# Part of the second head group's V made during the recurrences, with five context chunks and a fifth weight slot

## The chip, the cores and the metric

The kernel runs on one core of one Trainium2 chip. The metric is the device time of one execution in microseconds, the median of several. Lower is better.

## The reference, cut to what matters

Four layers follow each other on x (8 batches, 112 steps, 512 channels) with a context ctx (8 batches, 375 rows, 512 channels), all in float32. The first is a recurrence with gates and a feed-forward part; the second two cross-attentions and an MLP; then latents and a last attention. The change touches the first layer's recurrence and the first cross-attention:

```python
# layer 0, per batch: 32 heads of 16 channels, a state s of 16 x 16 per head
def step(s, rkvw):
    r_t, k_t, v_t, w_t = rkvw
    a = k_t[:, :, :, None] * v_t[:, :, None, :]
    out = jnp.einsum('bhk,bhkd->bhd', r_t, u * a + s)
    return (a + w_t[:, :, :, None] * s, out)
...
# layer 1: 16 heads of 128 channels; kv_in is ctx, the same for both attentions
qh = (q_in @ wq + bq).reshape(b, q_len, H, K)
kh = (kv_in @ wk + bk).reshape(b, t, H, K)
vh = (kv_in @ wv + bv).reshape(b, t, H, K)
kh = concatenate([kh, bias_k]); vh = concatenate([vh, bias_v])
weights = softmax(einsum('bqhk,bthk->bhqt', qh, kh) / scale)
return einsum('bhqt,bthk->bqhk', weights, vh) @ wo + bo
```

V depends on the context and a weight alone, not on x.

## The kernel before, in words

Matrices are multiplied in three passes of single-rate float32 (`mm3`, line 187: high x high, low x high, high x low), so each operand is kept as a high and a low part. A weight of 512 x 512 (1 MB) comes into one raw tile, ACT casts it to its high part in two halves (`act_split_weight`), POOL subtracts to get the low part (`pool_split_weight`, line 229), and both lie in one of `NSLOT` = 4 slots. `ORDER` lists the weights in the order of use, `SLOT` the slot of each; a load waits until the weight before it is split.

**The recurrences.** The batches are taken in two halves of four. In each half a loop of 64 steps (n) runs over four groups of channels, 16 steps each. In a step VectorE multiplies k by a broadcast row of v (`dve_outer`; in twelve steps POOL does it, `POOL_OUTER`) and scans the state over time (`dve_scan`, line 1127), POOL multiplies the state by r (`pool_read`, line 1306), and TensorE (PE) places the results, two steps at a time, in a bank (`pe_place`, line 685). ACT puts the first state in place (`act_init`, line 908). The v rows come by DMA from HBM, broadcast, into six tiles (`sp_spread`), issued six steps ahead by SyncE (SP), whose queue carries all of these transfers. Every engine goes through the steps in an order written out by hand: between steps stand the late products of k and r, the gate's (`GATE_AT`), the norm's transposes (`TURN_AT`), sums over heads, and the weights' splits at n = 9, 18 and 59. In the loop of 64 steps the read of step n waits for the placing of step n - 4, and the outer product and the scan's first state for the read of step n - 4.

**The fills.** In steps 13 to 60 of both halves PE also makes V of the first head group of the attention (`pe_fill`). A *fill* is one group and one batch, 376 rows of context by 512 columns, in three tiles of up to 128 rows (`KTILES`), and each tile adds over four chunks of the context. A *quantum* is one tile and one chunk: three matmuls of 512 columns. There are 12 quanta in a fill, 4 fills in a half, one quantum in each of the 48 steps. `QUANTA` gives their order: tile 0 over its four chunks, then tiles 1 and 2 together, chunk by chunk. The tiles use banks 0 and 1 in turn; ACT copies a full one to SBUF (`act_value_out`, line 427) and SP stores it to HBM (`sp_value_store`, line 457). The chunks, 188 KB for each part, lie in weight slot 3 (`CONTEXT_SLOT`), one place for each of four, and are loaded from `cx_dram` by `sp_chunk` (lines 450 and 451), once the fill before has read that place. POOL made that split of the context before the loop (`pool_cx`).

**The first attention.** 32 units, one for each of four head groups and eight batches, then as many for the second attention. `unit_steps` writes PE's order: keys of four heads, the turned probabilities of the unit before, then V's three tiles (36 matmuls of 512 columns) with the attended rows and the output product between them, then the logits. Where `made(n)` holds (the first group), the unit has no V matmuls; SP brings V back from HBM (`sp_made_values`), the logits stand on both sides of the attended rows, and V's bias is added to the attended rows (`act_attended`, `dve_attended`) by four instructions in place of one.

## Time and profile before

| | us |
|---|---|
| median of 3 runs | 3144.73 |
| lowest, highest run | 3142.94, 3148.15 |
| span of the profiled execution | 3143.0 |
| PE busy in it | 2966.0 (94%) |
| loop of the first half, first scan to last | 96.7 to 232.6 |
| loop of the second half | 311.3 to 448.3 |
| first attention, first head group | 580.3 to 743.0 |

The span runs from the first to the last instruction of the profiled execution. Which of the three runs it was is not given; its span lies 0.1 us above the lowest run and 1.7 below the median.

### The profile page before, as it was taken

The numbers are of one execution on the slowest core, as the hardware profiler recorded it, in microseconds if no ns is written. First come the engines' busy times: TensorE is split into PE (matmuls) and PEld (weight loads), VectorE is DVE, ScalarE is ACT, GpSimd is POOL, SyncE is SP. The second block draws the span as 40 slices with busy tenths as digits, with TensorE's granted clock in tenths as the row PEclk, the third lists the DMA queues.
The fourth block names the chain that finished last, engine by engine and source line by source line (L and its number), as shares of the span: only waits on it lengthen the run. The fifth ranks groups of instructions, "written<-read, shape, count | busy, mean of one in ns | idle before, by whom it ended". The sixth has DMA issues, their size and how long they took to land.

```text
span 3143.0 us, 43370 instructions
## 1 busy us (share of the span) xinstructions
PE 2966.0 (94%) x16412; PEld 2488.1 (79%) x16412; DVE 1326.3 (42%) x3062; ACT 1117.2 (36%) x2541; POOL 1030.7 (33%) x956
## 2 busy tenths in 40 slices
PE   6799888899999999999999999999989999998999
PEld 3445456888998998888989989989878877777887
DVE  4784886433333333433333333333421156563134
ACT  2333345433223222333232222232333355564332
POOL 4674674213113122222121121131245333345420
PEclk8897899999999999999999999999999999999999
DMA  6664651532122122222122222121111111111133
GB/s 214 188 195 164 199 165 44 195 119 106 60 73 106 60 73 87 73 76 78 70 93 74 73 80 73 67 106 60 53 41 67 66 45 45 43 38 58 54 114 94
DMA packets 98260, 289.75 MB, mean 92 GB/s; under 512 B 8552, under 2 KB 55144, under 8 KB 89224
## 3 DMA queue, kind: packets, MB, share of 16 engines
q1 hardware_dynamic: 97576, 286.29, 26.8%
q8 instruction: 134, 2.20, 0.3%
q10 hardware_dynamic: 480, 0.69, 0.1%
q14 instruction: 70, 0.57, 0.1%
HBM read 262.96 MB, written 23.99 MB: 91 GB/s over the span
## 4 chain that ended last, share of the span: by engine, by line
PE 74%; DVE 7%; ACT 6%; POOL 5%; issue 4%; DMA 3%; PEldq 0%; PEld 0%; SPq 0%; ACTq 0%; POOLq 0%; DVEq 0%
PE bank L189 21%; PE bank L191 20%; PE bank L190 20%; PE bank L1908 5%; POOL W_lo L229 3%; PE bank L1893 2%; DMA W_raw<-in_weights 2%; DVE max L2118 1%; ACT W_hi L220 1%; ACT prob L1996 1%; PE bank L2537 1%; DVE prob L2747 1%; PE bank L625 1%; POOL x L1306 1%; ACT prob L2652 1%
## 5 line engine op out<-in xcount | busy, mean ns | idle before, releaser
L2202 POOL TENSOR_SCALAR prob<-prob,inverse 112x376 f32<-112x376 f32 x256 | 144.3, 584 | 1275.1 <-DVE inverse L2124 1275.1
L229 POOL TENSOR_TENSOR W_lo<-W_raw,W_hi 128x1024 fp32r<-128x1024 f32 x138 | 329.1, 2408 | 159.7 <-ACT W_hi L220 156.1
L189 PE MATMUL bank<-ctx_hi,W_hi 128*128 128x376 f32 x1024 | 354.0, 346 | 6.8 <-DVE K_lo L271 4.2
L271 DVE SCALAR_TENSOR_TENSOR K_lo<-bank,vectors,K_hi 128x375 fp32r<-128x375 f32 (+1 forms) x288 | 172.8, 606 | 408.7 <-ACT K_hi L262 408.7
L190 PE MATMUL bank<-ctx_lo,W_hi 128*128 128x376 f32 x1024 | 343.7, 336 | 0.0
L191 PE MATMUL bank<-ctx_hi,W_lo 128*128 128x376 f32 x1024 | 343.2, 335 | 0.0
L189 PE MATMUL bank<-act_hi,W_hi 128*128 128x448 f32 x784 | 300.1, 383 | 10.5 <-DVE act_lo L269 3.6
L2069 DVE TENSOR_TENSOR V<-bank,bv 128x512 f32<-128x512 f32 x168 | 116.3, 692 | 433.6 <-PE bank L1908 235.4
L1996 ACT ACTIVATE prob<-bank,minus 112x376 f32<-112x376 f32 x256 | 143.7, 574 | 434.3 <-DVE minus L2121 434.3
L190 PE MATMUL bank<-act_lo,W_hi 128*128 128x448 f32 x784 | 293.2, 374 | 0.0
L191 PE MATMUL bank<-act_hi,W_lo 128*128 128x448 f32 x784 | 292.7, 373 | 0.0
L189 PE MATMUL bank<-W_hi,ctx_hi 128*128 128x512 f32 (+1 forms) x672 | 274.0, 408 | 3.1 <-DVE K_lo L271 3.1
L190 PE MATMUL bank<-W_lo,ctx_hi 128*128 128x512 f32 (+1 forms) x672 | 265.4, 395 | 0.0
L191 PE MATMUL bank<-W_hi,ctx_lo 128*128 128x512 f32 (+1 forms) x672 | 264.5, 394 | 0.0
L262 ACT ACTIVATE K_hi<-bank,vectors 128x375 fp32r<-128x375 f32 (+1 forms) x288 | 162.8, 577 | 218.2 <-PE bank L191 218.2
L189 PEld LDWEIGHTS bank<-ctx_hi,W_hi 128*128 128x128 f32 x1024 | 193.4, 189 | 11.6 <-DVE K_lo L271 8.2
L189 PEld LDWEIGHTS bank<-act_hi,W_hi 128*128 128x128 f32 x784 | 151.8, 194 | 53.8 <-issue 31.7
L190 PEld LDWEIGHTS bank<-ctx_lo,W_hi 128*128 128x128 f32 x1024 | 193.9, 189 | 0.4
L191 PEld LDWEIGHTS bank<-ctx_hi,W_lo 128*128 128x128 f32 x1024 | 193.5, 189 | 0.0
L1908 PEld LDWEIGHTS bank<-prob_T,V 128*128 128x128 f32 (+1 forms) x1536 | 180.8, 191 | 8.8 <-DVE prob_T L2075 3.9
L1908 PE MATMUL bank<-prob_T,V 128*128 128x112 f32 (+1 forms) x1536 | 181.4, 275 | 1.9 <-DVE prob_T L2075 1.9
L190 PEld LDWEIGHTS bank<-act_lo,W_hi 128*128 128x128 f32 x784 | 151.9, 194 | 14.1 <-issue 0.4
(278 smaller groups left out, 6124.1 us busy)
## 6 DMA issues: line engine op xcount, KB each, us to landing
W_raw<-in_weights SPq DMA_DIRECT2D x69, 1024.0 KB, 4.9
ctx_hi<-ctx_split SPq DMA_DIRECT2D x64, 752.0 KB, 4.3
ctx_lo<-ctx_split SPq DMA_DIRECT2D x64, 752.0 KB, 5.8
v_spread<-v_rows SPq DMA_DIRECT2D x88, 224.0 KB
att<-in_ctxT SPq DMA_DIRECT2D x16, 376.0 KB, 5.3
ctx_split<-W_hi SPq DMA_DIRECT2D x16, 376.0 KB, 3.9
ctx_split<-W_lo SPq DMA_DIRECT2D x16, 376.0 KB, 4.9
W_hi<-ctx_split SPq DMA_DIRECT2D x32, 188.0 KB, 4.3
```

What stands on the lines that cost most here:

```text
L189: nc.tensor.matmul(dst, left[0], right[0], start=first, stop=False)
L190: nc.tensor.matmul(dst, left[0], right[1], start=False, stop=False)
L191: return nc.tensor.matmul(dst, left[1], right[0], start=False, stop=last)
L220: act.copy(k.Wh[:, slot, cs, :], k.Wraw[:, cs, :]).then_inc(*k.w_high.now((n, i)))
L229: pool.tensor_tensor(k.Wl[:, slot, cs, :], k.Wraw[:, cs, :], k.Wh[:, slot, cs, :].bitcast(F32), ALU.subtract).then_inc(*k.w_low.now((n, i)))
L262: act.activation(high, src, ACT.Identity, bias=bias).then_inc(*k.banks.halving(key))
L271: dve.scalar_tensor_tensor(out=low, in0=src, scalar=bias, in1=high.bitcast(F32), op0=ALU.add, op1=ALU.subtract).then_inc(*k.banks.draining ...
L1893: m = pe.transpose(bank[0:kn, j * T:(j + 1) * T], k.Pm[:, h, k0:k0 + kn], k.ident[0:T, 0:T])
L1908: m = pe.matmul(bank[:, h * T:(h + 1) * T], k.Vt[0:kn, j, h * P:(h + 1) * P], k.PT[0:kn, h, j, :], start=j == 0, stop=j == 2)
L1996: act.activation(k.Pm[:, h, :], k.banks.tile(key)[0:T, 0:SP], ACT.Exp, bias=k.nb[:, h:h + 1], scale=SCALE1, accum_out=k.ssum[:, h:h + 1]). ...
L2069: dve.tensor_tensor(k.Vt[0:kn, j, :], k.banks.tile(key)[0:kn, :], k.bv[0:kn, j // 2, :], ALU.add).then_inc(*k.banks.draining(key))
L2202: pool.tensor_scalar(k.Pm[:, h, :], k.Pm[:, h, :], k.rsum[:, h:h + 1], 1.0, ALU.mult, ALU.mult).then_inc(*k.prob_done.now((n, h)))
```

## The change

MADE becomes 2, and `WHOLE` = 1 is the number of groups made for all batches. V of group 1 is made for batches 2, 3, 6 and 7, so a half has six fills: group 0 of batches 0 and 1, then both groups of 2 and of 3 (4 to 7 in the second half). The first two go at one quantum per step in steps 13 to 36, the others at two in steps 37 to 60. The order of quanta is now tile by tile. The context has five places in slot 3, used in rotation over batches and chunks, and each batch's chunks are loaded once for both groups; a chunk is released by the last tile of the last group. ACT and SP follow PE as before for copies; SP stores a tile one step later than ACT copies it, and loads chunks in PE's own step. Group 1's weight is loaded ahead of the first loop and split in steps 3 and 5, into slot 4, and kept; the gate's load of the first half moves into step 5, behind it. That weight is loaded again in the attention for the four units that still make V. `dynamic_dma_scratch_size=512` is given when the program is built.

```diff
-MADE = 1
-ORDER = (["v", "k", "r", "v1_0", "g", "o", "v", "r", "k"] + [f"v1_{g}" for g in range(1, MADE)] + ["g", "o", "fr", "fk"]
+MADE, WHOLE = 2, 1
+ORDER = (["v", "k", "r"] + [f"v1_{g}" for g in range(MADE)] + ["g", "o", "v", "r", "k", "g", "o", "fr", "fk"]
...
-NSLOT = 4
+NSLOT = 5
...
-SLOT = ([0, 1, 0, 2, 1, 0, 1, 1, 0] + [2] * (MADE - 1) + [0, 1, 0, 2]
-        + [3, 1, 0, 2] + [(n + 3) % NSLOT for n in range(len(ORDER) - ORDER.index("q1_1"))])
+SLOT = ([0, 1, 0] + [2, 4] + [1, 0, 1, 1, 0] + [0, 1, 0, 2]
+        + [3, 1, 0, 2] + [(n + 3) % 4 for n in range(len(ORDER) - ORDER.index(f"q1_{WHOLE}"))])
...
-FILLS = [(g, b) for g in range(MADE) for b in range(B)]
-QUANTA = [(0, c) for c in range(C)] + [(j, c) for c in range(C) for j in (1, 2)]
+def groups_of(b):
+    return 1 if b % HB < 2 else MADE
+
+FILLS = [(g, b) for b in range(B) for g in range(groups_of(b))]
+QUANTA = [(j, c) for j in range(3) for c in range(C)]
...
-QUANTA_AT = [MADE if FILL_FROM <= n < FILL_TO else 0 for half, n in POINTS]
+QUANTA_AT = [groups_of((n - FILL_FROM) // NQ) if FILL_FROM <= n < FILL_TO else 0 for half, n in POINTS]
...
+CHUNKS = 5
+
+def chunk_slot(b, c):
+    return (C * (b % HB) + c) % CHUNKS
...
+def context_chunk(k, b, c):
+    cols = slice(SP * chunk_slot(b, c), SP * (chunk_slot(b, c) + 1))
+    return [w[:, CONTEXT_SLOT].rearrange("p c d -> p (c d)")[:, cols] for w in (k.Wh, k.Wl)]
...
 def tiles_of(quanta):
-    f, q = divmod(quanta, NQ)
-    return 3 * f + (q >= 4) + (q >= 11)
+    return quanta // C
...
-        elif j == 2:
-            m.then_inc(*k.chunk_read.now((f, c)))
+        elif j == 2 and g == groups_of(b) - 1:
+            m.then_inc(*k.chunk_read.now((b, c)))
...
 def sp_fill(k, half, n):
-    for q in range(made_until((half, n), 2), made_until((half, n), 1)):
+    for q in range(made_until((half, n), 1), made_until((half, n))):
         f, q = divmod(q, NQ)
-        j, c = QUANTA[q]
-        if j == 2 and (f + 1) % PER_HALF:
-            sp_chunk(k, f + 1, c)
-    for t in range(tiles_of(made_until((half, n), 3)), tiles_of(made_until((half, n), 2))):
+        (j, c), (g, b) = QUANTA[q], FILLS[f]
+        if q == 0 and g == 0 and (b + 1) % HB:
+            sp_chunk(k, b + 1, 0)
+        if j == 2 and g == groups_of(b) - 1 and (b + 1) % HB and c < C - 1:
+            sp_chunk(k, b + 1, c + 1)
+    for t in range(tiles_of(made_until((half, n), 2)), tiles_of(made_until((half, n), 1))):
         sp_value_store(k, t)
...
+def chunk_before(b, c):
+    i = C * (b % HB) + c - CHUNKS
+    return (b // HB * HB + i // C, i % C) if i >= 0 else None
...
+VALUES_AT = (3, 5)
...
+            if half == 0 and n in VALUES_AT:
+                act_split_weight(k, W_VALUES[1], (VALUES_AT.index(n),))
...
+            if half == 0 and n in VALUES_AT:
+                pool_split_weight(k, W_VALUES[1], (VALUES_AT.index(n),))
...
             sp_load_weight(k, W_VALUES[0])
             sp_cx_pass(k, 4, 8)
+            sp_load_weight(k, W_VALUES[1])
...
-        sp_load_weight(k, w["g"])
+        if half:
+            sp_load_weight(k, w["g"])
...
+            if half == 0 and n == VALUES_AT[1]:
+                sp_load_weight(k, w["g"])
...
 def made(n):
-    return n < MADE * B
+    return UNITS[n] in FILLS
...
-        pe.wait_ge(k.vt_loaded, 32 * (n + 1))
+        pe.wait_ge(k.vt_loaded, 32 * (made_before(n) + 1))
...
-    nc = _bacc.Bacc("TRN2", target_bir_lowering=False, num_devices=1)
+    nc = _bacc.Bacc("TRN2", target_bir_lowering=False, num_devices=1, dynamic_dma_scratch_size=512)
```

## Rows read from the trace of the kernel before

**Rows 1.** The page, its first part.
```profile
PE 2966.0 (94%) x16412; PEld 2488.1 (79%) x16412; DVE 1326.3 (42%) x3062; ACT 1117.2 (36%) x2541; POOL 1030.7 (33%) x956
```
**Rows 2.** Busy time by stretch of the recurrences; columns as in the first line.
```profile
core 0: us, PE busy (x) PEld busy (x) DVE busy (x) ACT busy (x) POOL busy (x), PEclk, DMA share, GB/s
...
118.46:178.40 59.94, 46.51 (x172) 23.70 (x172) 50.81 (x77) 19.59 (x54) 40.41 (x36) 0.89 0.64 195
178.40:226.60 48.20, 44.53 (x195) 24.84 (x193) 43.73 (x59) 24.07 (x59) 38.28 (x35) 0.96 0.62 193
...
396.89:443.90 47.01, 42.70 (x187) 24.04 (x186) 42.91 (x59) 22.84 (x56) 36.69 (x34) 0.96 0.62 198
```
**Rows 3.** PE's waits, 178.4 to 226.6, then 396.9 to 443.9: total, times, longest.
```profile
PE bank L189 <- DMA W_lo<-ctx_split: 3.2, 2, 1.9
...
PE bank L189 <- DMA W_lo<-ctx_split: 3.8, 2, 2.8
```
**Rows 4.** Busy time by stretch, first and third group of the first attention.
```profile
580.30:743.00 162.70, 154.15 (x914) 144.78 (x913) 60.10 (x199) 67.70 (x186) 37.23 (x46) 0.98 0.38 133
966.90:1188.80 221.90, 220.34 (x1237) 199.89 (x1236) 74.65 (x189) 63.23 (x152) 46.12 (x50) 1.00 0.21 78
```
**Rows 5.** Timeline of PE in the first recurrence, two quanta in a row: start, duration.
```profile
173.76 0.39 PE L191 MATMUL bank<-W_hi,W_lo 128*128 128x512 f32 x1
173.99 0.40 PE L189 MATMUL bank<-W_hi 128*120 128x512 f32 x1
```
**Rows 6.** Timeline of PE in the third group: twelve matmuls of a V tile.
```profile
1033.28 0.40 PE L189 MATMUL bank<-W_hi,ctx_hi 128*120 128x512 f32 x1
...
1036.06 0.36 PE L189 MATMUL bank<-act_hi,W_hi 128*128 128x448 f32 x1
```
**Rows 7.** PE's waits in the first group, 590 to 745.
```profile
PE bank L189 <- DVE K_lo L271: 4.2, 4, 2.3
PE bank L189 <- POOL W_lo L229: 2.6, 1, 2.6
PE bank L1908 <- DVE prob_T L2075: 1.9, 7, 0.3
PE bank L189 <- DVE o_lo L2083: 0.9, 3, 0.3
```
**Rows 8.** A split on POOL (lines, 96 to 119), and the timelines of POOL and VectorE.
```profile
L229 POOL TENSOR_TENSOR W_lo<-W_raw,W_hi 128x1024 fp32r<-128x1024 f32 x2 | 4.7, 2392 | 0.0
...
116.75 2.08 POOL L1306 TENSOR_TENSOR x<-tmp,rT 128x448 f32<-128x448 f32 x2
...
115.02 1.09 DVE L1127 TENSOR_TENSOR_SCAN state<-bank,state 128x452 f32<-128x452 f32 x1
```
**Rows 9.** Weight loads issued at 90.22 and 116.82: KB, us to landing.
```profile
W_raw<-in_weights SPq DMA_DIRECT2D x1, 1024.0 KB, 5.0
...
W_raw<-in_weights SPq DMA_DIRECT2D x1, 1024.0 KB, 11.5
```
**Rows 10.** Low parts of chunks: the one of 179.08, and the eight of 168 to 212.
```profile
W_lo<-ctx_split SPq DMA_DIRECT2D x1, 188.0 KB, 8.1
...
W_lo<-ctx_split SPq DMA_DIRECT2D x8, 188.0 KB, 6.7
```
**Rows 11.** Busy time of the stretch behind the wait at 187.24.
```profile
188.10:191.50 3.40, 3.40 (x9) 1.62 (x9) 1.42 (x3) 3.31 (x8) 1.20 (x2) 0.50 0.53 200
```
**Rows 12.** Timeline of PE about steps 26, 27 and 37 of the first half.
```profile
158.58 0.76 PE L189 MATMUL bank<-W_hi 128*128 128x512 f32 x1 [4.33 <-ACT value_rows L427]
...
163.65 1.21 PE L685 MATMUL bank<-y,place 128*32 128x448 f32 x4
...
178.62 0.95 PE L685 MATMUL bank<-x,place 128*32 128x448 f32 x4
```
**Rows 13.** Timeline of PE at the end of the second half: the last three placings.
```profile
444.75 0.94 PE L685 MATMUL bank<-x,place 128*32 128x448 f32 x4
449.39 0.95 PE L685 MATMUL bank<-y,place 128*32 128x448 f32 x4 [3.70 <-POOL y L1306]
451.80 1.71 PE L685 MATMUL bank<-x,place 128*32 128x448 f32 x4 [1.47 <-POOL x L1306]
```

More of the change, by code:

```diff
@@ L69 @@
 W_FFN = {w: ORDER.index(w) for w in ("fr", "fk", "fv")}
-W_X = [{w: ORDER.index(f"{w}{layer}_{g}") for w in ("qko" if layer == 1 and g < MADE else "qkvo")}
+W_X = [{w: ORDER.index(f"{w}{layer}_{g}", W_FFN["fv"]) for w in ("qko" if layer == 1 and g < WHOLE else "qkvo")}
        for layer in (1, 2) for g in range(G)]
@@ L217, in act_split_weight, with pool_split_weight @@
         act.wait_ge(*k.banks.filled(("vf", len(FILLS) - 1, 2)))
-    for i in range(2):
+    for i in parts:
         cs = slice(2 * i, 2 * i + 2)
         act.copy(k.Wh[:, slot, cs, :], k.Wraw[:, cs, :]).then_inc(*k.w_high.now((n, i)))
-def pool_split_weight(k, n):
+def pool_split_weight(k, n, parts=range(2)):
     if n >= len(ORDER):
@@ L225, in pool_split_weight @@
     pool, slot = k.nc.gpsimd, SLOT[n]
-    for i in range(2):
+    for i in parts:
         cs = slice(2 * i, 2 * i + 2)
@@ L442, in sp_first_chunk, with sp_chunk @@
             k.nc.sync.wait_ge(k.cx_stored[s], 32 * 4 * (half + 1))
-    sp_chunk(k, PER_HALF * half, c)
-def sp_chunk(k, f, c):
-    sp, b = k.nc.sync, f % B
-    if f % PER_HALF:
-        sp.wait_ge(*(k.chunk_read[f - 1, c] if c < C - 1 else k.banks.filled(("vf", f - 1, 2))))
-    ch, cl = context_chunk(k, c)
-    sp.dma_start(ch.bitcast(F32), k.cx_dram[b, 0, :, c]).then_inc(k.chunk_loaded[c], 16)
-    sp.dma_start(cl.bitcast(F32), k.cx_dram[b, 1, :, c]).then_inc(k.chunk_loaded[c], 16)
+    sp_chunk(k, HB * half, c)
+def chunk_before(b, c):
+    i = C * (b % HB) + c - CHUNKS
+    return (b // HB * HB + i // C, i % C) if i >= 0 else None
+def sp_chunk(k, b, c):
+    sp, before = k.nc.sync, chunk_before(b, c)
+    if before:
+        b0, c0 = before
+        sp.wait_ge(*(k.chunk_read[before] if c0 < C - 1 else k.banks.filled(("vf", FILLS.index((groups_of(b0) - 1, b0)), 2))))
+    ch, cl = context_chunk(k, b, c)
+    sp.dma_start(ch.bitcast(F32), k.cx_dram[b, 0, :, c]).then_inc(k.chunk_loaded[chunk_slot(b, c)], 16)
+    sp.dma_start(cl.bitcast(F32), k.cx_dram[b, 1, :, c]).then_inc(k.chunk_loaded[chunk_slot(b, c)], 16)
 def sp_value_store(k, n):
@@ L1774, in made, with made_before, value_units @@
 def made(n):
-    return n < MADE * B
+    return UNITS[n] in FILLS
+def made_before(n):
+    return sum(made(m) for m in range(n))
+def value_units(gg):
+    return [n for n in range(8 * gg, 8 * gg + 8) if not made(n)]
 def unit_steps(n):
@@ L2249, in sp_xattn @@
     sp_made_values(k, 0)
[L2250 removed]
+    sp_value_bias(k, WHOLE)
     sp_context(k, 1)
@@ L2254, in sp_xattn @@
     for n, (gg, b) in enumerate(UNITS):
-        if b == 0 and gg > MADE:
+        if b == 0 and gg > WHOLE:
             sp_value_bias(k, gg)
@@ L3247, in semaphores @@
     k.zeroed, k.first_zeroed = sem("zeroed"), sem("first_zeroed")
-    k.chunk_loaded, k.vb_loaded = [sem(f"chunk_loaded{c}") for c in range(C)], [sem(f"vb_loaded{i}") for i in range(SPREADS)]
+    k.chunk_loaded, k.vb_loaded = [sem(f"chunk_loaded{c}") for c in range(CHUNKS)], [sem(f"vb_loaded{i}") for i in range(SPREADS)]
     k.value_kept, k.v_kept = [sem("value_kept0"), sem("value_kept1")], [sem(f"v_kept{i}") for i in range(4)]
```

35 lines of the change are left out of this document (18 added, 17 removed).

## The prediction

> **What bounds the kernel now.** I began with the page: TensorE (PE) is busy 94% of a span of 3143.0 us [rows 1]. That is an average, and the change only touches two stages, so I read each by itself. The metric is the median of the runs, 3144.73 us; the profiled execution is summed against its span, 3143.0 us, which lies 1.7 us below that median, and I carry the difference through. About 0.2% (6.3 us) is what a measurement of this kernel can tell from no change.
>
> *The two recurrences* are read in busy time by stretch [rows 2], cut at the scans of steps 13, 37 and 61. In steps 13 to 36 (59.94 us in the first half) VectorE is busiest, 50.81 us, against PE's 46.51. In steps 37 to 60 (48.20 and 47.01 us), where the change adds its work, PE is busy 44.53 and 42.70 us, and what it waits for there is nearly all one thing, the low part of a context chunk: 3.2 us in the first half, 3.8 in the second [rows 3]. So there is almost no hole in PE into which a second quantum per step could go.
>
> *The first attention* (512 keys by 4 heads, eight groups of heads, eight batches each) is read by comparing the group whose V is already made (the first, 162.70 us in that stretch) with one that makes its own (the third, 221.90 us): PE is busy 154.15 and 220.34 us [rows 4]. Both are PE's; the made group has more idle time.
>
> **What the change moves, and what it costs.** One quantum is three matmuls of 512 columns. When one quantum follows another on PE, the matmuls start 0.23 us apart even across the border (173.76, then 173.99) [rows 5], so one more quantum in a step costs 0.70 us. The change adds 24 in steps 37 to 60 of each half: 24 x 0.70 = 16.8 us per half, **+33.6 us**, since PE is full there and becomes the bound by a wide margin (44.5 + 16.8 = 61.3 us against VectorE's 43.7).
>
> In the attention four units of the second group (batches 2, 3, 6, 7) lose 36 such matmuls each. There twelve of them in a row take 1033.28 to 1036.06, 0.232 us each [rows 6]: 36 x 0.232 = 8.35 us, four times, **-33.4 us**. The matmuls thus cancel, and the sum is made of the waits.
>
> (1) *Made units have less cover.* In the first group PE waits 1.9 us in 7 pieces for the turned probabilities, 4.2 us for the low keys, 0.9 us in 3 pieces for the attended rows and 2.6 us for a weight's low part [rows 7]; the third group's stretch is idle for 221.90 - 220.34 = 1.6 us in all [rows 4]. For four made units I take four pieces of the first (1.1), four of the third (1.2), two short ones of the second (0.9), and at the end of the group (batch 7 is made, as in the first group) the weight wait of 2.6 and 0.9 behind it in place of those 1.6 (1.9), plus 1.7 us for one more stretch at half clock, as the first group's PEclk of 0.98 over 162.70 us shows two such, 3.3 us of lost clock [rows 4]. **+6.8 us**; bounds 3 (the waits without weight and clock) and 8.5 (all of the first group's idle time, 162.70 - 154.15, for half as many units).
>
> (2) *The early split.* The weight for group 1's V is split in steps 3 and 5 of the first recurrence, and the load of the gate's weight moves behind it, to step 5 of SyncE's queue, where it waits for the second part of the split. ACT has room for the two copies. POOL does not: half a split takes 2.39 us [rows 8], and from step 4 on its reads pile up. Step by step: its read and outer product of step 3 end at 104.6; the half split, reads 4 and 5 (1.07 us each) and the other half end at 111.4, and reads 6 to 9 follow without a hole, to 115.5. The gate's load can be issued only at 111.4, where before it went out ahead of the loop; 1 MB lands 5.0 us after issue when the queue is empty and 11.5 when it is in traffic [rows 9]. ACT waits for it in step 9 and splits to 119, so that scan 12 starts at 119.3 against 115.02, and POOL's read 10 at 122.8 against 116.75 [rows 8]. The spreads queued behind that wait on SyncE land late as well (that of step 13 at about 122). VectorE has no hole until step 17 in which to take it back. **+4.3 us**, in the first half alone; bounds 1 (what POOL adds, less VectorE's idle) and 6.1 (read 10).
>
> (3) *Chunks.* Before, a chunk's slot was free four steps before its next use and PE still waited [rows 3]. Now three of four chunks of the next batch are released only by the last tile of the last group, and their use comes five quanta later. With two quanta a step that is two steps. From the release of the last chunk to its use I count, at the passage from one quantum a step to two (steps 35 to 38): the rest of step 36 0.8 us, a placing of 0.87, a gate product of 0.6 and three quanta, 3.7 us after the placing, so 4.5 in all. At the passage from batch 2 to 3 (steps 48 to 50) it is 5.3 us. The low part of a batch's last chunk lands 8.1 us after its issue (some 0.4 us after the release), and 6.7 us is the median of eight [rows 10]. That gives waits of about 4.0 and 3.0 us, 7.0 per half, against 3.2 and 3.8 now: +3.8 and +3.2. I add 1 us per half for one more stretch at half clock: after the wait of 1.9 us PE ran at 0.50 of its clock (1.2 GHz) for 3.4 us [rows 11]. **+9.0 us**; bounds 0 and 15. By the Trainium skill (DMA: Bandwidth & Descriptors, Anatomy of one DMA — SWDGE (gpsimd) path) a software-issued transfer takes about 2.0 us and its bytes at 436 GB/s, by which I estimate 2.4 us for 188 KB; nothing would then wait, and this term would be -7.0. The trace disagrees by a factor of three for these SyncE copies in traffic, and the measurement decides.
>
> (4) *What it gives back.* The old order began tile 2 one quantum after tile 0 was full, and PE stood 4.3 us for ACT's copy at step 26, and then ran at half clock: 0.76 us for the next matmul, where 0.40 is usual [rows 5, 12]. In the new order each bank has four quanta to be emptied. The placing of step 27, at 163.65, then comes at about 158.5, when ACT is through with the same step's table loads and root (PE's wait ended at 158.58); VectorE sets the pace to step 37, whose placing comes at 174.7 instead of 178.62 [rows 12]. **-3.9 us per half, -7.8**; bounds -2 and -10. At the end of the loop the other engines are ahead of PE. In the second half the last three placings stand at 444.75, 449.39 and 451.80, with 3.7 and 1.5 us of waiting [rows 13]; POOL's split now lies under PE's steps 57 to 60, and the last placing ends 3.9 us after that of step 61 instead of 8: -4.0. In the first half the low-rank products fill that place: -0.7. **-4.7**; bounds -1.4 and -6.
>
> The other edits cost nothing that lasts: six more value copies on ACT per half (24.07 of 48.20 us busy there [rows 2]) and six stores on SyncE, covered while PE is the bound; SyncE now waits for PE's own step before it issues the spread seven steps ahead, and VectorE can lead PE by six steps at most, so without that lead the spreads would be what is late. One weight more is loaded.
>
> Sum: 33.6 - 33.4 + 6.8 + 4.3 + 9.0 - 7.8 - 4.7 = **+7.8 us**: a span of 3150.8 and a time of **3152.5 us**.
>
> **Rivals.** *A, the chunks come in time* (the load on the queue per us falls as the steps get longer): term 3 is about 0, so 7.8 - 9.0 = -1.2, 3143.5 us. For it: the share of the DMA engines, 0.62 in steps 37 to 60 [rows 2], leaves room. Against: the 8.1 us was measured at that share.
> *B, the waits shrink everywhere*, the side of faster: PE's order without its hole at step 26 is what decides; it wins if term 3 is 0 and terms 1 and 2 are at their lower bounds: 0.2 + 3 + 1 - 7.8 - 4.7 = -8.3, 3136.4 us. The point from which it decides: added waits of terms 1 to 3 together under 6.3 us.
> *C, PE has room after all.* PE's weight loads are busy only 24.84 of 48.20 us in steps 37 to 60, against 199.89 of 221.90 in the attention [rows 2, 4]. If the loads measured its load, 16.8 us would fit into the 23 left and the whole -33.4 us would be gained: 3152.5 - 33.6 = 3118.9. The Trainium skill says so (Perfetto Trace Analysis, Identifying the Most-Contended Engine: the busy share of the weight loads tells headroom, that of matmuls does not). Against it: these matmuls are wide, starts are 0.23 us apart back to back, and the weight loads wait under them [rows 5].
> *D, ACT is late with the tiles* at two quanta per step, as at step 26 before: it has two table loads in each of steps 40 and 56. One such wait of 4.3 us and its slow clock per half: +12, 3165 us. Against: a bank now has two steps, about 5 us.
>
> **Chances.** Forecast 0.48 (of it a fifth inside 0.2%), A 0.24, B 0.14, C 0.03, D 0.11. Faster: B and C, 0.17. Within 0.2% (3138.4 to 3151.0): A and a fifth of the forecast, with little of B, 0.34. Slower: 0.49. Range 3138 to 3165: down to just below A, leaving out most of B and C, and up to D, which also holds the forecast with term 3 at its upper bound.
>
> **What would show it.** Per half, steps 37 to 60 should last 64 to 67 us with PE over 90% busy; a wait for W_lo<-ctx_split of some 7 us; no wait for ACT value_rows at step 26; scan 12 of the first half about 4 us later after the start of its loop; the second group of heads about 26 us shorter, its made units with 0.3 us waits; the second half's loop about 4 us shorter at its end. I am wrong if those steps grow by much less than 17 us, or if the chunk waits stay at 3 us.

## The result, and the profile after

The changed kernel takes **3149.23 us** (median of 16 runs, 3144.70 to 3156.74), the kernel before 3141.74 us over the 16 runs taken beside it: a ratio of 1.0025, 95% interval 1.0018 to 1.0032, or 7.8 us slower (the two medians lie 7.5 us apart). It is slower beyond its interval; whether by more than 0.2% the interval leaves open. One thousandth in a ratio is 3.14 us in what follows. Four executions of the runs below took far longer than their kernels' others (3324, 3690, 4141 and 10074 us): the ratios leave them out, the medians given count them, and without them would be at most 1.0 us lower. The profiled execution spans 3147.0 us, only 4.0 more than the 3143.0 before, so the two traces show about half of the 7.8 us. The page gives PE a little more busy time and VectorE a little less than [rows 1]:

```profile
PE 2974.4 (95%) x16412; PEld 2490.0 (79%) x16412; DVE 1312.0 (42%) x3071; ACT 1127.7 (36%) x2576; POOL 1033.7 (33%) x958
```

The totals hide what happened. I set the same events of both traces side by side: the first scan of a loop, PE's placings of steps 37 and 61 and the last placing of a half, and in the attention ACT's first key copy.

```
                              before     after    difference   grown since the row above
half 1, first scan              96.70     95.88      -0.8        -0.8
        placing 37             178.62    186.67      +8.1        +8.9
        placing 61             225.72    251.72     +26.0       +17.9
        last placing           235.50    259.76     +24.3        -1.7
half 2, first scan             311.34    334.46     +23.1        -1.1
        placing 37             397.10    418.01     +20.9        -2.2
        placing 61             444.75    484.42     +39.7       +18.8
        last placing           451.80    488.54     +36.7        -2.9
attention, first key copy      580.27    613.76     +33.5        -3.3
```

Busy time by stretch of the changed kernel, cut at the scans of steps 13 (first half), 37 and 61, columns as in [rows 2]:

```profile
125.21:186.45 61.24, 51.08 (x170) 24.57 (x168) 51.54 (x77) 20.23 (x53) 38.73 (x34) 0.80 0.63 193
186.45:249.38 62.93, 58.07 (x253) 36.28 (x252) 42.10 (x59) 25.71 (x62) 38.26 (x35) 0.97 0.56 177
417.80:481.49 63.69, 58.89 (x251) 36.46 (x249) 41.51 (x59) 25.71 (x62) 38.14 (x36) 0.95 0.55 173
```

PE is now the busiest engine of steps 37 to 60 by 16 us (58.07 against VectorE's 42.10; 44.53 against 43.73 in [rows 2]). The stretches last 14.7 and 16.7 us longer than in [rows 2], where they are cut at VectorE's scans; cut at PE's placings, as in the table, they grow by 17.9 and 18.8, since by step 61 VectorE has run ahead of PE (by 2.3 us in the first half, where it was 0.9 behind). PE's waits for the low part of a chunk from placing 37 to placing 61, first and second half (3.2 and 3.8 in [rows 3]):

```profile
PE bank L189 <- DMA W_lo<-ctx_split: 4.8, 2, 2.5
...
PE bank L189 <- DMA W_lo<-ctx_split: 4.7, 2, 2.5
```

Busy time of the first attention, the first three groups of heads in the changed kernel, and then the second group in the kernel before, columns as above:

```profile
613.80:775.10 161.30, 152.72 (x906) 143.41 (x905) 60.08 (x199) 67.60 (x187) 37.08 (x46) 0.98 0.38 135
775.10:968.90 193.80, 189.47 (x1093) 174.11 (x1092) 69.16 (x198) 66.63 (x173) 45.99 (x50) 0.99 0.30 105
968.90:1193.00 224.10, 223.83 (x1260) 203.41 (x1258) 75.95 (x193) 63.89 (x156) 46.15 (x50) 1.00 0.21 77
```

```profile
743.00:966.90 223.90, 222.68 (x1252) 202.03 (x1250) 75.86 (x193) 63.80 (x155) 46.19 (x50) 1.00 0.21 77
```

The second group is 30.1 us shorter, the first 1.4 shorter, the third 2.2 longer than in [rows 4], all of that in its first unit: together -29.3 us. PE's waits in the second group are of three of the four kinds that were expected; waits for low keys didn't come:

```profile
PE bank L189 <- POOL W_lo L229: 2.4, 1, 2.4
PE bank L1946 <- DVE prob_T L2113: 1.1, 4, 0.3
PE bank L189 <- DVE o_lo L2121: 0.6, 1, 0.6
```

**The early split** costs more than the forecast had. Timeline of VectorE in the changed kernel, the first and last columns being the start and the idle time before the instruction with what ended it:

```profile
118.52 0.62 DVE L1143 TENSOR_TENSOR state<-v_spread,bank 128x448 f32<-128x448 f32 x1 [3.13 <-DMA v_spread<-v_rows]
119.06 1.09 DVE L1153 TENSOR_TENSOR_SCAN tmp<-bank,tmp 128x452 f32<-128x452 f32 x1
121.82 0.62 DVE L1143 TENSOR_TENSOR state<-v_spread,bank 128x448 f32<-128x448 f32 x1 [1.68 <-DMA v_spread<-v_rows]
122.36 1.09 DVE L1153 TENSOR_TENSOR_SCAN state<-bank,state 128x452 f32<-128x452 f32 x1
124.67 0.62 DVE L1143 TENSOR_TENSOR tmp<-v_spread,bank 128x448 f32<-128x448 f32 x1 [1.22 <-DMA v_spread<-v_rows]
```

The scan of step 12 starts at 122.36, where it was at 115.02 [rows 8]; counted from the loop's first scan it is 8.2 us late, and scan 13 is 7.6 late. Up to scan 13 VectorE waits 6.0 us for three spreads in a row, two of them ahead of scan 12, where it waited for none. For POOL's reads it waits 2.9 us, where it waited 1.8. So most of the delay is the spreads'. SyncE's queue shows why; its timeline in the changed kernel, and the same issue of a spread in the kernel before:

```profile
102.08 0.57 SPq L1426 DMA_DIRECT2D wT<-v_rows  x1
110.54 0.35 SPq L206 DMA_DIRECT2D W_raw<-in_weights  x1
110.93 0.57 SPq L1432 DMA_DIRECT2D mx<-v_rows  x1
111.54 0.58 SPq L1426 DMA_DIRECT2D v_spread<-v_rows  x1
```

```profile
103.52 0.56 SPq L1404 DMA_DIRECT2D mx<-v_rows  x1
104.64 0.57 SPq L1398 DMA_DIRECT2D v_spread<-v_rows  x1
```

The load of the gate's weight stands until 110.54 for POOL's second half split, and the spreads behind it go out 6.9 us late, together with the 1 MB load and eight chunk transfers.

**The hole at step 26** has gone, as expected, and another has come. Timeline of PE about steps 27, 32 and 37 of the first half:

```profile
166.14 0.60 PE L748 MATMUL bank<-ident,head_root 112*128 112x112 f32 x4 [1.43 <-ACT head_root L960]
166.68 0.57 PE L709 MATMUL bank<-y,place 128*32 128x448 f32 x2
...
176.94 0.98 PE L238 MATMUL bank<-ident,normalised 112*128 112x112 f32 x4 [2.45 <-DVE normalised L1083]
...
186.67 0.57 PE L709 MATMUL bank<-x,place 128*32 128x448 f32 x2
```

Against 163.65 and 178.62 in [rows 12], placing 27 is 3.0 us later and placing 37 is 8.1 later: what the order gave at step 26 (some 4 us, after the split had cost 8 by step 13) is lost again within ten steps.

### The profile page after: what moved, and what is told of

Read it like the earlier page. It is cut to its first block, busy times and chain, and to the rows that moved or that the text cites. A ratio compares the mean times of both kernels' runs of the same rounds, so it can differ in the third digit from the quotient of the medians.

```text
span 3147.0 us, 43434 instructions
## 1 busy us (share of the span) xinstructions
PE 2974.4 (95%) x16412; PEld 2490.0 (79%) x16412; DVE 1312.0 (42%) x3071; ACT 1127.7 (36%) x2576; POOL 1033.7 (33%) x958
## 4 chain that ended last, share of the span: by engine, by line
PE 77%; DVE 7%; ACT 5%; POOL 4%; issue 4%; DMA 3%; SPq 0%; PEldq 0%; PEld 0%; POOLq 0%; ACTq 0%; DVEq 0%
PE bank L189 22%; PE bank L190 21%; PE bank L191 21%; PE bank L1946 6%; POOL W_lo L229 2%; PE bank L1931 2%; DMA W_raw<-in_weights 1%; DVE max L2156 1%; PE bank L709 1%; ACT prob L2034 1%; PE bank L2575 1%; ACT W_hi L220 1%; DMA W_lo<-ctx_split 1%; PE bank L649 1%; DVE prob L2785 1%
## 5 line engine op out<-in xcount | busy, mean ns | idle before, releaser
L2107 DVE TENSOR_TENSOR V<-bank,bv 128x512 f32<-128x512 f32 x156 | 107.9, 692 | 399.3 <-PE bank L1946 217.5
L189 PE MATMUL bank<-W_hi,ctx_hi 128*128 128x512 f32 (+1 forms) x624 | 254.5, 408 | 3.1 <-DVE K_lo L271 3.1
L190 PE MATMUL bank<-W_lo,ctx_hi 128*128 128x512 f32 (+1 forms) x624 | 246.5, 395 | 0.0
L191 PE MATMUL bank<-W_hi,ctx_lo 128*128 128x512 f32 (+1 forms) x624 | 245.6, 394 | 0.0
L189 PE MATMUL bank<-W_hi 128*128 128x512 f32 (+2 forms) x368 | 154.6, 420 | 10.8 <-DMA W_lo<-ctx_split 10.3
```

Of the source, the lines that this page charges most:

```text
L189: nc.tensor.matmul(dst, left[0], right[0], start=first, stop=False)
L190: nc.tensor.matmul(dst, left[0], right[1], start=False, stop=False)
L191: return nc.tensor.matmul(dst, left[1], right[0], start=False, stop=last)
L2107: dve.tensor_tensor(k.Vt[0:kn, j, :], k.banks.tile(key)[0:kn, :], k.bv[0:kn, j // 2, :], ALU.add).then_inc(*k.banks.draining(key))
```

## Experiments

Twelve kernels, in three sets of four, each set on one chip beside runs of the kernel before (medians 3142.72, 3140.58 and 3142.93 us). I compare ratios across sets, never raw times. The difference of two ratios has a 95% interval of about 0.0013, or 4 us, to either side (an estimate from the intervals of the two), and each price below is to be read with it. The names in the expectations are the kernels'; they stand in brackets below. By *lag* I mean how many steps SyncE's queue puts a store or a chunk load behind the step that releases it: the change made both lags one step shorter.

### The new order alone, with the new and with the old lags

The split had been measured in the trace, but the loss between placings 27 and 37 could come from the order of the quanta or from SyncE's queue. Both kernels leave the second group out of the recurrences and load the gate's weight before the loop (e1_order); the second also restores the old lags (e2_order_lags). Both keep the new order, the five chunks, the fifth slot and `dynamic_dma_scratch_size=512`.

```diff
-MADE, WHOLE = 2, 1
+MADE, WHOLE = 1, 1
...
-        if half:
-            sp_load_weight(k, w["g"])
+        sp_load_weight(k, w["g"])
```
and in the second, in `sp_fill`:
```diff
-    for q in range(made_until((half, n), 1), made_until((half, n))):
+    for q in range(made_until((half, n), 2), made_until((half, n), 1)):
...
-    for t in range(tiles_of(made_until((half, n), 2)), tiles_of(made_until((half, n), 1))):
+    for t in range(tiles_of(made_until((half, n), 3)), tiles_of(made_until((half, n), 2))):
```

> The changed kernel without its second group's work: one quantum per step, one weight (v1_0), the gate's weight loaded ahead of the loop as before; what is left of the change is the order of the quanta, the five context chunks and SyncE's new lags. Theory S (SyncE's new lags make the spreads of steps 28 to 32 late, so that what the order gives at step 26 is gone by step 37): placing 27 about 5 us earlier against the start of the loop, placing 37 at most 1 us earlier in each half; with a chunk now free five steps before its use the waits for chunks shrink by 1 to 3 us per half; in all -2 to -7 us, 3135 to 3140. Rival, as the prediction had it: placing 37 is 3.9 us earlier in each half and with the shorter chunk waits in all -10 to -14 us, 3128 to 3132. Second rival, the order is worth nothing by itself: within 2 us of before.

> As e1_order, but with SyncE's old lags: chunk loads one step later in its queue and the stores of the made tiles one step later, so that SyncE never waits for the step's own PE or ACT work. Theory S: the v_spread loads of steps 28 to 32 are in time, the gain of step 26 stays to step 37, 2 to 4 us per half less than e1_order, 4 to 8 us in all; some of it is given back if the chunks come a step later. Rival (the relief is lost to VectorE's and POOL's own pace, whatever SyncE does): within 2 us of e1_order.

Measured: new lags 3144.99 us, ratio 1.0011 (1.0002 to 1.0020); old lags **3135.63 us**, 0.9981 (0.9972 to 0.9990). Both sizes that the expectation gave a gain for the first were too low: with SyncE's new lags the order doesn't gain. That it is worth nothing, the second rival, lies inside the interval. The lags alone are worth 0.0030, 9.4 us, more than theory S allowed. In both traces placing 27 of the first half comes 5.1 us earlier against the loop's first scan, as the forecast had it; by placing 37 there is 1.0 us left of it (1.9 in the second half) with the new lags, 2.3 (2.9) with the old, where the forecast had 3.9. VectorE's waits for broadcast loads from about step 23 of the second half on, new lags, then old:

```profile
DVE tmp L1141 <- DMA v_spread<-v_rows: 2.0, 2, 1.6
DVE state L1141 <- DMA v_spread<-v_rows: 1.6, 1, 1.6
...
DVE tmp L1141 <- DMA th<-v_rows: 0.3, 1, 0.3
```

```profile
DVE tmp L1141 <- DMA th<-v_rows: 1.1, 1, 1.1
DVE state L1141 <- DMA v_spread<-v_rows: 0.3, 1, 0.3
DVE tmp L1141 <- DMA v_spread<-v_rows: 0.2, 1, 0.2
```

3.9 us against 1.6; before step 23 the two differ by 0.6 us the other way, and in the first half by 0.6. The direction is the one of theory S; that late spreads are the way by which the lags cost 9.4 us isn't shown, since these waits hold 2.3 us of it and the two profiled executions are only 4.7 us apart where the medians are 9.4 apart (the one with the new lags was the shortest of its 11 runs).

### Is it the order or the fifth chunk?

The better kernel of the two with four chunks (e9_order_four):

```diff
-CHUNKS = 5
+CHUNKS = 4
...
-        if q == 0 and g == 0 and (b + 1) % HB:
-            sp_chunk(k, b + 1, 0)
-        if j == 2 and g == groups_of(b) - 1 and (b + 1) % HB and c < C - 1:
-            sp_chunk(k, b + 1, c + 1)
+        if j == 2 and g == groups_of(b) - 1 and (b + 1) % HB:
+            sp_chunk(k, b + 1, c)
```

> As e2_order_lags with four context chunks instead of five. Theory O (the gain of e2_order_lags comes from the order: a bank has four quanta to be emptied, so PE doesn't stand at step 26): within 2 us of e2_order_lags, 3134 to 3138. Rival, the fifth chunk is what gains: the waits for chunks come back to the 3 to 4 us per half of before and the time is 3140 to 3142.

Measured: 3145.73 us, 1.0010 (1.0001 to 1.0018). Theory O falls, and the time lies beyond the rival's too. PE's waits for chunks from about step 24 on in the first half, with five chunks and with four:

```profile
PE bank L189 <- DMA W_lo<-ctx_split: 3.1, 2, 1.6
```

```profile
PE bank L189 <- DMA W_lo<-ctx_split: 9.5, 8, 1.9
```

The order frees the banks early but the chunks late: with four slots it reads each chunk for the last time four quanta before its slot is needed, where the old order left seven, six, five and four. So the order is worth nothing without the fifth chunk (which makes 0.0029, 9 us), and the two together, with the old lags, are worth 6 us. No run has the fifth chunk with the old order, or the fifth slot and the scratch size by themselves, so what those give alone is open.

### The early split, taken out and added alone

First the changed kernel with the split moved to steps 27 and 29, its load to step 20 and the gate's load back ahead of the loop (e3_late_split), then the same with the stores one step later in SyncE's queue (e5_late_split_store):

```diff
-VALUES_AT = (3, 5)
+VALUES_AT = (27, 29)
...
+        sp_load_weight(k, w["g"])
...
-                sp_load_weight(k, W_TIME[1]["v"] if half == 0 else W_FFN["fr"])
+                sp_load_weight(k, W_VALUES[1] if half == 0 else W_FFN["fr"])
+            if n == 31 and half == 0:
+                sp_load_weight(k, W_TIME[1]["v"])
```

> The changed kernel with the split of v1_1 moved from steps 3 and 5 to steps 27 and 29 of the first recurrence (its load to step 20, the next v weight's to step 31, the gate's load back ahead of the loop). Theory E (the early split and the late gate load cost the first half 8 us, which nothing later takes back, since PE follows these scans): scan 13 at its old distance from the start of the loop, in all -6 to -9 us against the changed kernel, 3140 to 3143, no longer measurably slower than before. Rival M (the split's price moves with it: ACT and POOL are late in steps 27 to 32 instead, where the changed kernel already waits): scan 13 early, but placing 37 at most 4 us earlier than in the changed kernel, in all -1 to -4 us. Rival, as the prediction had it: 4.3 us.

> As e3_late_split, and the stores of the made tiles one step later in SyncE's queue, as before the change, so that SyncE doesn't stand behind ACT's copy of the same step at step 25. Theory S: 2 to 4 us per half less than e3_late_split, 3133 to 3139, and faster than before. Rival (the spreads are late from traffic, not from SyncE's waits): within 2 us of e3_late_split.

Measured: 3142.73 us, 1.0004 (0.9996 to 1.0013), and with the later stores **3138.23 us**, 0.9984 (0.9976 to 0.9993). The late split gives back 0.0021, 6.6 us, inside theory E's range, and the stores' lag another 0.0020, 6.3 us. In the traces, counted from the first half's first scan, placing 27 comes 9.0 us earlier with the late split and placing 37 8.2 earlier, so rival M falls; but steps 37 to 61 then last 69.6 us in place of 65.1, with longer waits for chunks and a lower clock, and by the last placing 3.7 us are left. The second is faster than the kernel before and 13 us faster than the changed one, with the same work moved.

The other way round, the early split without any quantum that uses it (e7_split_alone):

```diff
 def groups_of(b):
-    return 1 if b % HB < 2 else MADE
+    return 1
```

> As e1_order (new order, new lags, one quantum per step), with the second v weight loaded, split in steps 3 and 5 of the first recurrence and the gate's weight loaded behind it, as in the changed kernel, but no quantum uses that weight. Theory E (the early split is the first half's loss by itself): 7 to 9 us above e1_order, all of it there by step 13 and still there at the end of the half; 3152 to 3154. Rival, the prediction's size: 4.3 us, 3149. Rival R (where PE isn't full in steps 37 to 60, VectorE and POOL take part of it back): scan 13 is 7 us late, but at the end of the half under 4 us are left.

Measured: 3152.95 us, 1.0035 (1.0025 to 1.0045): 0.0024 or 7.5 us above the order alone. Theory E again, and rival R falls: against that kernel's trace scan 13 is 6.8 us late, and the last placing of the half 12.1. VectorE stands at the same place and for the same spreads as in the changed kernel:

```profile
119.22 0.62 DVE L1143 TENSOR_TENSOR state<-v_spread,bank 128x448 f32<-128x448 f32 x1 [2.99 <-DMA v_spread<-v_rows]
...
122.83 1.09 DVE L1153 TENSOR_TENSOR_SCAN state<-bank,state 128x452 f32<-128x452 f32 x1
```

### When the chunks are asked for

The late split with both old lags (e6_late_both_lags), and with the old chunk lag in the single steps only (e14_hybrid):

```diff
-    for q in range(made_until((half, n), 1), made_until((half, n))):
+    for q in range(made_until((half, n), 2), made_until((half, n), 1)):
```
```diff
+def chunks_until(half, n):
+    return made_until((half, n), 0 if QUANTA_AT[POINTS.index((half, n))] == MADE else 1)
...
-    for q in range(made_until((half, n), 1), made_until((half, n))):
+    for q in range(chunks_until(half, n - 1), chunks_until(half, n)) if n > FILL_FROM else ():
```

> As e5_late_split_store, and the chunk loads one step later in SyncE's queue too, as before the change. Theory S (nothing in SyncE's queue may wait for the step's own work): 2 to 4 us less than e5_late_split_store, 3134 to 3137. Rival (in the double steps, where the chunks are already late, one step later costs more than the queue gains): waits for chunks 2 to 5 us per half longer than in e5_late_split_store, in all 3 to 8 us more, 3141 to 3146. Against e2_order_lags, which does the same without the second group's work, the difference is the net price of that work: by the prediction's terms 6.8 (less cover) + 9.0 (chunks) + 0.2 - 4.7 (loop end) = +11, by what the traces of the changed kernel showed about +3 to +6.

> As e5_late_split_store, with the chunk loads one step later in SyncE's queue (as before the change) in the single steps 13 to 36 and not in the double steps 37 to 60. Theory L (the two halves of the lag have opposite signs: where chunks have five steps it is the queue that counts, where they have two and a half it is the chunk): steps 13 to 36 as in e2_order_lags, placing 37 some 1 to 2 us earlier per half than in e5_late_split_store, the double steps as there: 3134 to 3137. Rival (in single steps the chunk lag does nothing, and e6_late_both_lags lost its 9 us in the double steps alone): as e5_late_split_store, 3138.

Measured: 3147.35 us, 1.0013 (1.0003 to 1.0024), and 3140.08 us, 0.9992 (0.9983 to 1.0000). The first is 9.1 us above the kernel with the later stores alone: in the double steps a chunk that is asked for one step later costs more than the queue gains, the rival. The waits of the two traces show only part of it (8.8 us of chunk waits in the double steps of both halves, against 11.0). PE's clock shows much of the rest. These are the double steps, placing 37 to placing 61 of each half, with the later stores alone and then with both old lags:

```profile
178.34:246.65 68.31, 62.95 (x261) 39.55 (x260) 44.77 (x63) 25.55 (x61) 40.82 (x37) 0.93 0.51 169
414.08:475.71 61.63, 58.22 (x261) 37.34 (x260) 44.00 (x61) 25.54 (x61) 40.59 (x36) 1.00 0.56 185
```

```profile
179.90:249.70 69.80, 63.82 (x262) 39.57 (x261) 44.58 (x62) 25.55 (x61) 40.72 (x36) 0.90 0.49 161
415.01:482.50 67.49, 62.38 (x262) 38.93 (x261) 44.77 (x62) 25.98 (x62) 41.33 (x37) 0.92 0.51 166
```

They last 7.4 us longer, and the granted clock is 0.90 and 0.92 where it was 0.93 and 1.00. But single traces don't settle this: the next section's first kernel has the same first half as the one with both old lags, and its double steps there last 64.2 us at 0.97, not 69.8 at 0.90.

The second kernel can't be told from the one with the later stores (intervals 0.9983 to 1.0000 and 0.9976 to 0.9993): what the chunk lag does in single steps stays open.

The changed kernel with four chunks (e4_four_chunks) tests the forecast's wait itself; its edit is that of the four-chunk kernel above, on the changed kernel.

> The changed kernel with four context chunks instead of five, so that each chunk's slot is free four quanta before its next use and not five. Theory C (PE waits for the landing: one quantum less is 1.3 us less in the double steps and 2 us in the single ones): waits for chunks of 8 to 12 us per half instead of 4.8, in all +6 to +12 us on the changed kernel, 3155 to 3161. Rival (the wait is for traffic and not for the slot's release, since the low part lands 6 to 8 us after its issue only in the burst of four): within 3 us of the changed kernel.

Measured: 3161.23 us, 1.0057 (1.0045 to 1.0069), 0.0032 or 10 us above the changed kernel: theory C. PE's waits for chunks from about step 24 on, first and second half, with four chunks and then with five:

```profile
PE bank L189 <- DMA W_lo<-ctx_split: 9.8, 8, 3.0
...
PE bank L189 <- DMA W_lo<-ctx_split: 9.8, 9, 2.4
```

```profile
PE bank L189 <- DMA W_lo<-ctx_split: 4.9, 3, 2.5
...
PE bank L189 <- DMA W_lo<-ctx_split: 5.4, 3, 2.5
```

The waits grow by 9.3 us in all and the time by 10, with 4 to either side: as far as these runs can tell, a wait is paid in full here.

### Where a second quantum is cheap, and what it gives back

In the second half the weight is there from the start, so the double steps can lie in steps 13 to 36, where PE isn't full. First on the kernel with the late split and both old lags (e11_half1_front):

```diff
-    return 1 if b % HB < 2 else MADE
+    return 1 if (b % HB < 2) == (b < HB) else MADE
...
-QUANTA_AT = [groups_of((n - FILL_FROM) // NQ) if FILL_FROM <= n < FILL_TO else 0 for half, n in POINTS]
+QUANTA_AT = [groups_of(HB * half + (n - FILL_FROM) // NQ) if FILL_FROM <= n < FILL_TO else 0 for half, n in POINTS]
```

> As e6_late_both_lags, but in the second half it is the first two batches (steps 13 to 36, where PE is busy only some 50 of 61 us) that are made for both groups, instead of the last two. Theory P (a quantum costs its 0.70 us only where PE is full): of the 16.8 us that the second quanta cost in that half 6 to 10 lie in PE's waits, 3127 to 3131. Rival (PE's waits in steps 13 to 36 are waits of a chain that runs through PE, so each added quantum delays the chain): within 3 us of e6_late_both_lags. Second rival: chunks are late there, since the passages come in the steps with the most traffic: slower than e6_late_both_lags.

Measured: 3144.04 us, 1.0008 (0.9999 to 1.0017), against 1.0013: not to be told apart, so theory P isn't borne out by the time. Its mechanism can be seen in the trace: steps 13 to 36 of the second half now last

```profile
353.48:423.48 70.00, 63.60 (x238) 36.74 (x239) 52.74 (x77) 22.74 (x61) 40.32 (x36) 0.90 0.59 190
```

70.00 us, 9.2 more than the 60.80 (357.00 to 417.80) of the changed kernel, for 16.8 us of matmuls. But making units 4 and 5 gives the attention 2.7 us less than making units 6 and 7 (second group and first unit of the third shrink by 25.3 us, not 28.0), and the gain at the loop's end is gone.

Then these two batches alone, with the weight split in steps 40 and 42 of the first half (e12_half1_only); the cut is against e14_hybrid:

```diff
+MADE_FOR = (4, 5)
...
-    return 1 if b % HB < 2 else MADE
+    return MADE if b in MADE_FOR else 1
...
-VALUES_AT = (27, 29)
+VALUES_AT = (40, 42)
```

> The second group's V made for batches 4 and 5 alone, in steps 13 to 36 of the second half; its weight split in steps 40 and 42 of the first half; lags as in e14_hybrid; the first half makes one quantum per step throughout. Theory P (the price of a second quantum is what PE's waits leave of its 0.70 us: in the traces 21 us per half in steps 37 to 60 of the first half, 10 in steps 13 to 36 of the second, against 12.7 us that two units give back in the attention): e2_order_lags less 2 to 4 us, 3131 to 3134, the fastest of all. Rival (no place in the recurrences is cheaper than the attention): e2_order_lags or above, 3136 to 3140.

Measured: 3141.33 us, 0.9995 (0.9986 to 1.0003), 0.0014 or 4 us above e2_order_lags: theory P misses, and the rival is nearer. Its profiled execution has the span of 3133.3 us that theory P asked for, and is the shortest of 12 runs that reach to 3148.43. One trace isn't a time.

Last, the cost without the return: V of the second group is made in the recurrences, and its units make it again (e10_units_make).

```diff
 def made(n):
 
-    return UNITS[n] in FILLS
+    return n < B
```

> The changed kernel with the second group's V made in the recurrences all the same, but not used: the four units make their own as before. It parts the change's cost (recurrences) from what it gives back (attention). The traces of the two kernels put the gain in the attention at 29.3 us, so 3149.2 + 29.3 = 3178.5 (3175 to 3182), and the recurrences' cost at 37 us. As the prediction had it: 33.4 - 6.8 = 26.6, 3175.8. Rival (the gain is read wrongly because the units around the made ones take part of it, or because the clock does): under 24 or over 33 us.

Measured: 3184.36 us, 1.0135 (1.0122 to 1.0148): 35 us above the changed kernel over four executions, more than either number and on the rival's side. Its second group lasts

```profile
776.70:1000.90 224.20, 223.92 (x1260) 203.43 (x1258) 75.95 (x193) 63.95 (x156) 46.22 (x50) 1.00 0.21 77
```

224.20 us, against 193.80 with the made values, and the two traces differ by 28 us up to the end of the third group's first unit. The rest lies elsewhere: 1.8 in the recurrences, which are the same in both, and 5.2 in later groups, where the change has no part; the last section shows them. Whether the three executions without a trace have them too isn't known.

## Why the prediction was right, and for the wrong reasons

The forecast was +7.8 us and so is the measurement (the forecast's 3152.5 us stands on a median of 3 runs that the 16 put 3.0 lower). But one of its steps came out beyond its bounds, another had been given no cost at all, and three others came out cheaper than forecast and made up for it. Added up as measured below, the terms make +6 to +10 us, depending on which runs price the split and the lags. That the errors cancel to a tenth of a us is luck. Of the signs that it had named, the chunk waits (4.8 against some 7), scan 12 (8.2 us late against 4) and steps 37 to 60 (62.9 and 63.7 us against 64 to 67) fell outside; the hole at step 26 is gone, as it said.

- **The matmuls** cancel. Steps 37 to 61 of PE grew by 17.9 and 18.8 us, of which 16.8 was the quanta's. Rival C is out: PE's weight loads were busy 24.84 of 48.20 us there before, and nothing of the 16.8 us fitted in beside them. Here the Trainium skill (Perfetto Trace Analysis, Identifying the Most-Contended Engine), which judges headroom by the busy share of the weight loads, beside the share of peak arithmetic that is reached, and the trace differ, and the measurement decides.
- **(1) Less cover**: +6.8 forecast. -29.3 us in the attention against -33.4 for the matmuls makes it **+4.1**, inside the bounds. The second group is idle for 4.3 us (193.80 - 189.47) where it was 1.2 before; the weight's wait (2.4) and the short waits for the probabilities (1.1) came as forecast, and a granted clock of 0.99 over 193.80 us shows the one more slow stretch. Of the waits for attended rows half came (0.6 of 1.2), and the 0.9 us for low keys that I took over from the first group didn't. The first group's 1.4 us is in part a matter of where it is cut: ACT's split of the next weight waits 6.47 us for the load where it waited 7.88, so ACT's first key copy of the second group comes 1.4 us earlier, while PE loses no more than a wait of 0.9 us for low keys just behind the cut (at 744.26 before).
- **(2) The early split**: +4.3 forecast, bound 6.1; **+7.5** by the kernel with the split alone, 6.6 by the one without it, each with 4 us to either side, and 7.6 us at scan 13 by the trace. The step that failed is "ACT waits for it in step 9 and splits to 119, so that scan 12 starts at 119.3". It followed POOL's backlog, which added 1.1 us to VectorE's waits up to scan 13; the spreads added 6.0. That the spreads behind the waiting load on SyncE are late was written down and given no price, and it was the longer path.
- **(3) Chunks**: +9.0 forecast. The waits are 4.8 and 4.7 us, not 7.0 each, and from placing 37 to placing 61 the two halves grew by 3.1 us beyond the quanta: **+3.1**. Where the same recurrences ran again, in e10_units_make, this stretch of the first half lasted 1.7 us longer, so that figure is no closer than this. The mechanism is right (four chunks: waits twice as long, +10 us), and the size is off at both ends. The step was "a placing of 0.87, a gate product of 0.6 and three quanta", and it left out the head sums (0.86 us, from 189.65): from the issue of the batch's last chunk at 186.43 to its use PE had 5.1 us of work, not 4.1. And the low part landed 7.46 us after its issue, the last one of the second passage 6.0, where I took 8.1 for both. PE's wait and the slow clock behind it, which answers to [rows 11]:

```profile
193.94 0.70 PE L189 MATMUL bank<-W_hi 128*128 128x512 f32 x1 [2.46 <-DMA W_lo<-ctx_split]
...
194.10:197.50 3.40, 3.40 (x8) 1.21 (x9) 2.37 (x4) 0.68 (x2) 0.72 (x2) 0.50 0.60 217
```

  The figure of the Trainium skill (DMA: Bandwidth & Descriptors, Anatomy of one DMA — SWDGE (gpsimd) path), by which I had estimated 2.4 us, is for transfers issued by GpSimd; these copies, issued by SyncE in traffic, landed 2.5 to 3 times later (6.0 and 7.46 us).
- **(4) The relief**: -7.8 forecast for step 26, and nothing for SyncE's lags. Placing 27 of the first half came 5.1 us earlier, as worked out, in every kernel with the new order, five chunks and no early split. The step that failed is "The other edits cost nothing that lasts", with its sentence on SyncE, which "now waits for PE's own step": those lags cost **9.4 us** with one quantum per step, and the stores' part 6.3 us in the kernel with the late split. With the old lags order and chunks are worth 6.0 us. I had credited 7.8 to the order alone; without the fifth chunk it gives nothing. So this term, -7.8 with nothing for the lags, was in the changed kernel some +0 to +3 (the 9.4 or the 6.3 less the 6.0, an estimate).
- **The loop's end**: -4.7 forecast. From placing 61 to the last one it is -1.7 and -2.9, **-4.6**. Another 3.3 us went before the attention's first key copy, unforeseen: after the last placing PE ran at half clock before (first row) and doesn't now (second), and the waits ahead of it had shrunk from 3.7 and 1.5 us [rows 13] to 0.2 and 2.0. That this is why the clock didn't fall is argued from the two traces and not tested.

```profile
451.80:458.00 6.20, 6.20 (x16) 3.50 (x16) 2.29 (x4) 1.06 (x2) 1.42 (x1) 0.52 0.04 16
```

```profile
488.54:494.74 6.20, 6.20 (x26) 4.03 (x27) 4.46 (x8) 1.93 (x4) 1.43 (x1) 1.00 0.29 120
```

Rival A, chunks in time, didn't come, though +3.1 is nearer to its 0 than to the forecast's +9.0. Rival B's condition, added waits under 6.3 us, wasn't met: terms 1 to 3 are 14.7. But the kernel with the late split and the later stores, which moves the same work, is 0.16% faster than before, so the faster side lay two small edits away. Rival D is out: in the double steps PE waits for chunks and for nothing else. Not settled are by what way the lags cost 9.4 us, and how much of the 9 us of a later chunk request is the clock's chance.

The two kernels that beat both are the late split with later stores (3138.23 us) and the new order with five chunks and no second group (3135.63 us). Their intervals overlap, so moving the second group's V is worth nothing that these runs show: what the recurrences pay is what the attention gives.

## What to carry to other kernels

When an edit makes a queue wait for the step's own work, price every transfer behind the waiting one, not only the engine that it waits for: both terms that the forecast had worst (the gate's load, the lags) lie there. For the gate's load the traces show the late spreads; for the lags the times show the price and the waits only a small part of it. Moving work between two stages that the same engine bounds gains nothing by itself; in these runs the waits at either end decided, so put the preparation (the split) and the requests where they block nobody before asking whether the move pays. And an order that frees one resource earlier (banks) may free another later (chunks): check both.

## What the runs showed that I hadn't expected

PE's clock can turn a small delay into a larger one. In the kernel whose units make V again, the wait for low keys at the start of the seventh and of the eighth group is longer than in the changed kernel, and the clock falls behind it. Timeline of PE at the seventh, then busy time and granted clock of the stretch behind it, and after them the same for the changed kernel:

```profile
1901.76 0.48 PE L1931 MATMUL bank<-ident,prob 112*128 112x112 f32 x3 [2.63 <-DVE K_lo L271]
...
1902.60:1906.00 3.40, 3.40 (x14) 3.31 (x13) 0.46 (x1) 0.14 (x2) 2.36 (x2) 0.51 0.28 70
```

```profile
1871.02 0.48 PE L1931 MATMUL bank<-ident,prob 112*128 112x112 f32 x3 [1.28 <-DVE K_lo L271]
...
1871.50:1875.00 3.50, 3.50 (x22) 3.33 (x23) 1.40 (x4) 1.45 (x3) 2.77 (x2) 1.00 0.27 51
```

A wait of 2.63 us is followed by 3.4 us at 0.51 of the clock (1.2 GHz), one of 1.28 us by none. The length of the wait alone doesn't decide: behind the one of 1.9 us at 187.24 in the kernel before the clock was 0.50 [rows 11], behind the one of 2.0 us ahead of the changed kernel's last placing it was 1.00. The longer wait comes twice in that trace, with a lengthening of the units on both sides of the passage by 1.2 to 1.6 us, and makes up the 5.2 us that the change can't explain. The same shows over many runs: of 32 runs of the kernel before in the second set, the nine with a mean granted clock of 0.973 or more average 3138.6 us, the eight with 0.970 or less 3143.9 us; beside the other two sets the same two groups lie 3.8 and 3.0 us apart. So one execution can lie 7 us below its kernel's median (3134.59 against 3141.33 us), and a difference of 3 us between two kernels of ten runs each told nothing here.
